# One batch's instruction order in an attention-block kernel: the TensorE, VectorE and ScalarE queues rewritten

## The chip, the cores and the metric

The kernel runs on 1 core of one Trainium2 chip. The metric is the device time of one execution in microseconds (us). Engines: PE is TensorE (PEld its weight loads), DVE is VectorE, ACT is ScalarE, POOL is GpSimd, SP is SyncE, which here only issues DMAs. Each engine works through its own instructions strictly in the order in which the program lists them; semaphores tie the engines together.

## The reference

Two layers over `x` of shape (32, 256, 256). Layer 0 is an attention block with an adaptive norm, layer 1 a response added to its output. Cut to what matters:

```python
# layer 0, B=32 batches, S=D=256, 16 heads of 16
emb = silu(_sin_emb(timestep)) @ W_ada + b_ada;  scale, shift = split(emb)
x = _ln(src) * (1 + scale) + shift
q, k, v = (x @ Wq + bq), (x @ Wk + bk), (x @ Wv + bv)          # 16 heads each
scores = q @ k.T / 4 + attention_bias                           # (32,16,256,256)
probs = softmax(where(src_mask, -inf, scores))
x = x + ((probs @ v) @ Wo + bo)
h = _ln(x) * g2 + beta2
x = x + (_gelu2(h @ W1 + b1) @ W2 + b2)                          # F=1024
# layer 1
U_o, V_o = gram_schmidt(U), gram_schmidt(V)                     # 32 columns each
basis = U_o @ V_o.T
strength = sigmoid(relu(mean(x) @ gate_w1.T + gate_b1) @ gate_w2.T + gate_b2) * sigmoid(safety)
out = x + strength * ((x @ basis) @ basis.T[:, :R] @ resp_w.T + resp_b + safety_bias)
```

## The kernel before

The kernel has two phases. Phase one runs the attention of the 32 batches, one batch per pass of a loop whose body each engine has written out for itself (`body(b, n)` in the blocks of vector, scalar and tensor; the first three and the last batches are unrolled, the middle ones are a hardware loop of two batches, `run_batches`, L110). It writes x after attention to DRAM (`x2_d`). Phase two (`body2`) runs the MLP and the response for the 32 batches. The change lies in phase one and in the last pass that leads over to phase two.

Work of one batch in phase one. Sequence rows lie in two tiles of 128 (qt, kt). Heads are handled one by one, 0 to 15; scores are made in groups of four heads.

- SP loads the attention bias of a batch in two chunks of eight heads into a ring of four slots (`load_bias`); chunk 1 of the next batch when the transposes of the batch before are done, chunk 0 of the batch after next when eight heads of this one are transposed (L315, L324).
- POOL adds the mask into the bias in the ring, in place, four heads at a time (`add_mask`, L430), normalises the x of the next batch (`inv_std`, `normalise_x`), and does parts of one Gram-Schmidt step per batch (`gs_norm`, `gs_update`); 32 batches make the 32 steps. Its order isn't changed.
- PE `scores(b, g)` (L1104) writes four heads' scores into four PSUM banks, which are single: a group waits until DVE has reduced all four heads of the group before. `transposes(b, h)` (L1117) turns the probabilities of head h into one of two PSUM banks (`tp_ps[h % 2]`) and waits for the copy of head h-2 and for head h's exponentials. `pv(b, g)` (L1132) multiplies four heads' transposed probabilities with v, into bank 6. Bank 6 also holds, in turn, the natural-layout context (`ctx_natural`, twice), its transpose (`ctx_transpose`) and the output projection (`project_o`); each of these waits for the eviction of the one before. Bank 7 (`prep_ps`) holds in turn the transposed x, Q, K, V and the transposed-back x of the next batch (`x_transpose`, `project_qk`, `project_v`, `x_back`), and the Gram products (`gs_gram`).
- DVE `reduce_head(b, h)` (L596) adds masked bias to scores, writes the sum to the ring and takes the row minimum of its negative; two instructions and two accumulator reads per head. It also evicts bank 7 (`xT_out`, `q_out` twice, `k_out`, `v_out`, `xres_out`), divides the context by the row sums (`normalise_ctx`, twice), adds the residual (`x2_out`), takes statistics of x (`stats`, `stats_end`), evicts the Gram products, and copies heads 3, 7 and 11 of the transposed probabilities (`copy_pT`, L609).
- ACT `exp_head(b, h)` (L872) does the exponentials in place, two instructions per head; `copy_pT(b, h)` (L879) copies the other 13 heads' transposed probabilities from PSUM to SBUF; `pv_out` and `ctxT_out` evict bank 6; `gs_coefficients`, `gs_write`, `gs_column` belong to the Gram-Schmidt step.

The order of each engine is written by hand as a loop over a slot h from 0 to 15, with one head's work per slot and fixed lags between engines (`behind(b, n, h, k)`, L103: the work of head h-k, reaching into the batch before): DVE reduces head h, ACT exponentiates head h-1, PE transposes head h-3, ACT or DVE copies head h-4. Everything else is hung on a slot number ("if h == 7"). What an engine does in the slot is what another waits for by semaphore count, so counts are independent of the order, and the order alone decides who stands in front of whom.

## Time and profile before

| | us |
|---|---|
| median of 3 runs (lowest, highest) | 1502.5 (1501.99, 1502.88) |
| the profiled execution itself | 1502.05 |
| its span, first to last instruction | 1499.9 |
| PE busy | 1369.4 (91%) |
| PE weight loads busy | 1129.5 (75%) |
| ACT busy | 1086.8 (72%) |
| DVE busy | 1065.5 (71%) |
| POOL busy | 870.4 (58%) |
| mean DMA rate over the span | 116 GB/s |

Phase one ends and phase two begins where the first MLP matmul starts, at 1016.83 us of the span. A matmul's recorded duration reaches to the modelled end of its result, which overlaps the next matmul in an unbroken run.

### The profile page before, as it was taken

The numbers are of one execution on the slowest core, as the hardware profiler recorded it, in microseconds if no ns is written. First come the engines' busy times: TensorE is split into PE (matmuls) and PEld (weight loads), VectorE is DVE, ScalarE is ACT, GpSimd is POOL, SyncE is SP. The second block draws the span as 40 slices with busy tenths as digits, with TensorE's granted clock in tenths as the row PEclk, the third lists the DMA queues.
The fourth block names the chain that finished last, engine by engine and source line by source line (L and its number), as shares of the span: only waits on it lengthen the run. The fifth ranks groups of instructions, "written<-read, shape, count | busy, mean of one in ns | idle before, by whom it ended". The sixth has DMA issues, their size and how long they took to land.

```text
span 1499.9 us, 39676 instructions
## 1 busy us (share of the span) xinstructions
PE 1369.4 (91%) x11998; PEld 1129.5 (75%) x11998; DVE 1065.5 (71%) x3539; ACT 1086.8 (72%) x2696; POOL 870.4 (58%) x874
## 2 busy tenths in 40 slices
PE   3899899999999899989998999989999999999997
PEld 3666666666666666666666666658999999999997
DVE  3667666766676666666666667657888888888775
ACT  1777777777777777777777777777777776777773
POOL 4997878787878787788878887722121212222110
PEclk9999999999999999999999999999999999999999
DMA  7545454545445454545454547200101010111100
GB/s 239 192 129 183 138 181 139 165 153 165 155 149 169 148 172 134 184 134 186 128 186 132 185 135 238 81 22 29 43 28 42 28 42 28 42 34 36 42 22 29
DMA packets 182766, 175.01 MB, mean 117 GB/s; under 512 B 15648, under 2 KB 182208, under 8 KB 182720
## 3 DMA queue, kind: packets, MB, share of 16 engines
q1 hardware_dynamic: 182720, 174.42, 36.7%
q8 instruction: 25, 0.41, 0.1%
q14 instruction: 21, 0.17, 0.0%
HBM read 157.63 MB, written 16.78 MB: 116 GB/s over the span
## 4 chain that ended last, share of the span: by engine, by line
PE 76%; DVE 12%; ACT 5%; issue 4%; SPq 1%; ACTq 1%; DVEq 0%; DMA 0%
PE bank L1323 13%; PE bank L1310 12%; PE bank L1114 9%; PE bank L1129 9%; PE bank L1172 8%; DVE ring L606 5%; PE bank L1152 4%; PE bank L1216 4%; PE bank L1179 4%; PE bank L1356 3%; ACT pT L882 2%; PE bank L1080 2%; ACT ring L877 2%; PE bank L1198 2%; DVE xT L618 2%
## 5 line engine op out<-in xcount | busy, mean ns | idle before, releaser
L430 POOL TENSOR_TENSOR ring<-ring,maskv 128x1024 f32<-128x1024 f32 x256 | 598.4, 2365 | 15.2 <-DMA ring<-in_fside 7.8
L877 ACT ACTIVATE ring<-ring,nmax 128x256 f32<-128x256 f32 x1024 | 458.5, 502 | 115.1 <-DVE nmax L606 112.7
L606 DVE CUSTOM_DVE_ANT_0 ring<-bank,ring 128x256 f32<-128x256 f32 x1024 | 385.5, 417 | 165.3 <-PE bank L1114 163.9
L1129 PE MATMUL bank<-ident,ring 128*128 128x128 f32 x2048 | 306.8, 278 | 26.4 <-ACT pT L882 26.4
L1129 PEld LDWEIGHTS bank<-ident,ring 128*128 128x128 f32 x2048 | 234.4, 142 | 95.2 <-ACT ring L877 42.1
L882 ACT ACTIVATE pT<-bank 128x512 f32<-128x512 f32 x416 | 243.1, 585 | 62.1 <-PE bank L1129 62.1
L984 ACT ACTIVATE work<-bank,b1t 128x256 f32<-128x256 f32 x256 | 107.5, 475 | 114.8 <-PE bank L1310 114.8
L1114 PE MATMUL bank<-work 32*128 32x256 f32 x2048 | 147.5, 402 | 26.3 <-DVE nmax L606 26.3
L1310 PE MATMUL bank<-hT_high,w_high 128*128 128x256 f32 x512 | 153.1, 299 | 3.0 <-DVE hT_rest L763 3.0
L1152 PE MATMUL bank<-pT,vt 128*32 128x256 f32 x2048 | 137.1, 385 | 14.5 <-ACT ctxT L892 13.9
L1323 PE MATMUL bank<-w_high,gT_high 128*128 128x256 f32 x512 | 147.9, 289 | 0.0
L1323 PE MATMUL bank<-w_rest,gT_high 128*128 128x256 f32 x512 | 144.4, 282 | 0.0
L1310 PE MATMUL bank<-hT_high,w_rest 128*128 128x256 f32 x512 | 144.2, 282 | 0.0
L1310 PE MATMUL bank<-hT_rest,w_high 128*128 128x256 f32 x512 | 144.2, 282 | 0.0
L1323 PE MATMUL bank<-w_high,gT_rest 128*128 128x256 f32 x512 | 144.2, 282 | 0.0
L779 DVE SCALAR_TENSOR_TENSOR pT<-work 128x512 f32<-128x512 f32 x128 | 89.3, 698 | 73.1 <-ACT work L988 59.5
L462 POOL TENSOR_SCALAR vpeb<-mvb 128x2 f32<-128x2 f32 x32 | 6.1, 191 | 226.8 <-DVE mvb L693 226.6
L1114 PEld LDWEIGHTS bank<-work 32*128 32x128 f32 x2048 | 92.9, 185 | 55.0 <-DVE nmax L606 41.4
L476 POOL TENSOR_TENSOR work<-work,b2b 128x512 f32<-128x512 f32 x32 | 41.6, 1300 | 131.8 <-DVE work L794 131.8
L1310 PEld LDWEIGHTS bank<-hT_high,w_high 128*128 128x128 f32 x512 | 96.9, 189 | 4.4 <-DVE x2s L662 2.3
L1152 PEld LDWEIGHTS bank<-pT,vt 128*32 128x32 f32 x2048 | 56.0, 109 | 57.9 <-issue 35.6
L376 POOL TENSOR_TENSOR nrm<-gii,expo 128x2 f32<-128x2 f32 x32 | 22.5, 704 | 130.3 <-DVE gsb L574 130.3
(158 smaller groups left out, 2851.2 us busy)
## 6 DMA issues: line engine op xcount, KB each, us to landing
ring<-in_fside SPq DMA_DIRECT2D x128, 1024.0 KB, 7.5
xt<-in_x SPq DMA_DIRECT2D x32, 256.0 KB, 7.8
x_d<-x2s SPq DMA_DIRECT2D x32, 256.0 KB, 7.8
work<-x_d SPq DMA_DIRECT2D x32, 256.0 KB, 2.7
out<-pT SPq DMA_DIRECT2D x32, 256.0 KB, 2.2
mk<-in_mask SPq DMA_DIRECT2D x32, 64.0 KB, 6.6
w<-in_W SPq DMA_DIRECT2D x2, 1024.0 KB, 10.8
wada<-in_W_ada SPq DMA_DIRECT2D x1, 512.0 KB, 4.0
```

Of the source, the lines that this page charges most:

```text
L430: nc.gpsimd.tensor_tensor(v, v, m, ALU.add).then_inc(s_masked, 1)
L606: nc.vector.tensor_tensor_reduce(out=v, in0=score_ps[h % HG][:, qt], in1=v, scale=-1.0, scalar=ROW_MAX_NEG, op0=ALU.add, op1=ALU.min, accu ...
L779: nc.vector.scalar_tensor_tensor(gT[:, 2 * j:2 * j + 2], th[:, j], 1.0, up[:, j], ALU.add, ALU.mult).then_inc(s2_g, 1)
L877: nc.scalar.activation(v, v, ACT.Exp, bias=nmax[:, b.par, h, qt:qt + 1], scale=-1.0).then_inc(s_exp, 1)
L882: nc.scalar.activation(pT[:, h % (2 * HG)], tp_ps[h % 2], ACT.Copy).then_inc(s_pta, 1)
L984: ins = nc.scalar.activation(th[:, j, f], tiles2(j)[:, f], ACT.Tanh, bias=b1t[:, 2 * j + f:2 * j + f + 1], scale=0.5 * GELU_A)
L1114: ins = mm(score_ps[r][:, qt], qm[rows, b.par, a, c, qt * P:(qt + 1) * P], kT[rows, b.par, c], start=True, stop=True)
L1129: ins = nc.tensor.transpose(tp_ps[h % 2][:, kt, qt * P:(qt + 1) * P], ring[:, slot, qt, h % CH, kt * P:(kt + 1) * P], ident[:])
L1152: ins = mm(pv_ps[VW * j:VW * (j + 1), :], vt[:, b.par, kt, h], pT[:, h % (2 * HG), kt], start=(kt == 0), stop=(kt == QT - 1))
L1172: ins = mm(prep_ps[:, n], w[:, c, n * P:(n + 1) * P], xT[:, c], start=(c == 0), stop=(c == DC - 1))
L1310: ins = mm(tiles2(j)[:, f], w1s[kw][:, c, n * P:(n + 1) * P], hTs[kx][:, b.par, c], start=(c == 0 and k == 0), stop=(c == DC - 1 and k == ...
L1323: ins = mm(tiles2(4)[:, t], gTs[kx][:, b.par, f, t * P:(t + 1) * P], w2s[kw][:, f], start=(f == 0 and k == 0), stop=(f == FC - 1 and k == ...
```

## The change

The three bodies (DVE, ACT, PE) are rewritten as straight lists; `behind` goes. What each function does and waits for is the same, and so is the number of instructions. Moved are:

- PE: x_transpose stands first in the batch, scores of group 1 behind head 0's transposes, group 2 behind head 5's, group 3 behind head 8's, group 0 of the next batch behind PV of group 1. The large projections lie between these. PV of group 2 is done at the end of the same batch; x_back stands ahead of the last head's transposes, and the output projection behind head 13's. All 16 heads' transposes are in the batch's own body.
- DVE: heads 0, 1, 2 of the next batch are reduced at the end of a body. The row maxima of a group come as soon as its scores are there, and evictions between them.
- ACT: exponentials of head 0 of the next batch stand in a body's end; copies are ahead of exponentials of heads further off (as copies 1 and 2 ahead of exponentials 4); gs_coefficients comes behind copy 4, gs_write behind exponentials 10.
- The last pass (n == B) has the same pieces in a new order: the output projection of the last batch now comes ahead of the transposes of phase two's first batch and of the last two steps of the response matrix.

```diff
--- before.py
+++ after.py
@@ DVE body @@
+            def reduces(b, heads):
+                for h in heads:
+                    reduce_head(b, h)
+
             def body(b, n):
-                for h in range(H):
-                    if main:
-                        reduce_head(b, h)
-                    at = behind(b, n, h, 4)
-                    if at and at[1] in DVE_HEADS:
-                        copy_pT(*at)
...
+                if n is None or n >= 2:
+                    x2_out(b.plus(-2))
+                if main:
+                    xres_out(b)
+                    if n is None or 1 <= n < B - 2:
+                        stats_end(b.plus(2))
+                    reduce_head(b, 3)
+                if prep:
+                    xT_out(b.plus(1))
+                if main:
+                    reduce_head(b, 4)
+                if tail:
+                    gs_reciprocal(b.plus(-1).n)
+                if main:
+                    reduces(b, (5, 6, 7))
+                    copy_pT(b, 3)
...
+                if prep:
+                    q_out(b.plus(1), 0)
+                    q_out(b.plus(1), 1)
+                if tail:
+                    normalise_ctx(b.plus(-1), 0)
+                if main:
+                    reduce_head(b, 8)
+                if tail:
+                    normalise_ctx(b.plus(-1), 1)
+                if main:
+                    reduce_head(b, 9)
+                if prep:
+                    k_out(b.plus(1))
+                if main:
+                    reduce_head(b, 10)
+                    copy_pT(b, 7)
+                    reduce_head(b, 11)
+                if prep:
+                    v_out(b.plus(1))
...
+                if main:
+                    reduces(b, (12, 13, 14, 15))
+                    gs_products(b)
+                    if n is None or n + 3 < B:
                         stats(b.plus(3))
+                    copy_pT(b, 11)
+                if prep:
+                    reduces(b.plus(1), (0, 1, 2))
...
@@ ACT body @@
+                if main:
+                    exp_head(b, 1)
+                    exp_head(b, 2)
+                    copy_pT(b, 0)
+                    exp_head(b, 3)
+                    copy_pT(b, 1)
+                    copy_pT(b, 2)
+                    exp_head(b, 4)
+                if tail:
+                    pv_out(b.plus(-1), 2)
+                if main:
+                    exp_head(b, 5)
+                if tail:
+                    pv_out(b.plus(-1), 3)
+                if main:
+                    exp_head(b, 6)
+                    copy_pT(b, 4)
+                if tail:
+                    gs_coefficients(b.plus(-1).n)
+                if main:
+                    exp_head(b, 7)
+                    exp_head(b, 8)
+                    copy_pT(b, 5)
+                    copy_pT(b, 6)
+                    exp_head(b, 9)
+                    pv_out(b, 0)
+                    exp_head(b, 10)
+                if tail:
+                    gs_write(b.plus(-1).n)
...
+                if main:
+                    gs_column(b.n)
+                    copy_pT(b, 8)
+                    exp_head(b, 11)
+                    copy_pT(b, 9)
+                if tail:
+                    ctxT_out(b.plus(-1))
+                if main:
+                    exp_head(b, 12)
+                    copy_pT(b, 10)
+                    exp_head(b, 13)
+                    pv_out(b, 1)
+                    exp_head(b, 14)
+                    exp_head(b, 15)
+                    copy_pT(b, 12)
+                    copy_pT(b, 13)
+                if prep:
+                    exp_head(b.plus(1), 0)
+                if main:
+                    copy_pT(b, 14)
+                    copy_pT(b, 15)
@@ PE body @@
+                if prep:
+                    x_transpose(b.plus(1))
+                if main:
+                    transposes(b, 0)
+                    scores(b, 1)
+                    transposes(b, 1)
+                    transposes(b, 2)
+                if prep:
+                    project_qk(b.plus(1), 0)
+                if main:
+                    transposes(b, 3)
+                if tail:
+                    pv(b.plus(-1), 3)
+                if main:
+                    transposes(b, 4)
+                    transposes(b, 5)
+                if tail:
+                    ctx_natural(b.plus(-1), 0)
+                if main:
+                    scores(b, 2)
+                if tail:
+                    ctx_natural(b.plus(-1), 1)
+                if prep:
+                    project_qk(b.plus(1), 1)
+                if main:
+                    pv(b, 0)
+                    transposes(b, 6)
+                    transposes(b, 7)
+                if prep:
+                    project_v(b.plus(1))
+                if main:
+                    transposes(b, 8)
+                    scores(b, 3)
+                    transposes(b, 9)
+                if tail:
+                    ctx_transpose(b.plus(-1), main)
+                if main:
+                    gs_gram(b, n)
+                    transposes(b, 10)
+                    transposes(b, 11)
+                    pv(b, 1)
+                if prep:
+                    scores(b.plus(1), 0)
+                if main:
+                    transposes(b, 12)
+                    transposes(b, 13)
+                if n == B:
+                    response_matrix(0)
+                if tail:
+                    project_o(b.plus(-1), main)
+                if n == B:
+                    y_transpose(Batch(0))
+                    response_matrix(1)
+                if main:
+                    transposes(b, 14)
+                if prep:
+                    x_back(b.plus(1), True)
+                if main:
+                    transposes(b, 15)
+                    pv(b, 2)
+                if n == B:
+                    response_matrix(2)
```

## Rows read from the trace of the kernel before

**Rows 1.** Busy time by stretch: us, then PE, PEld, DVE, ACT, POOL busy, clock, DMA.
```profile
500.00:530.30 30.30, 27.43 (x252) 20.51 (x252) 20.92 (x88) 22.75 (x57) 24.02 (x23) 1.00 0.50 158
...
1032.00:1499.00 467.00, 459.60 (x3802) 449.62 (x3801) 367.22 (x677) 334.52 (x862) 90.23 (x146) 0.99 0.11 34
```

**Rows 2.** Timeline of PE, scores of group 0: start, busy us, engine, line, operation.
```profile
90.66 1.15 PE L1114 MATMUL bank<-work 32*128 32x256 f32 x16
...
969.45 1.15 PE L1114 MATMUL bank<-work 32*128 32x256 f32 x16
```

**Rows 3.** Timeline of PE in one batch of the loop.
```profile
506.45 1.07 PE L1152 MATMUL bank<-pT,vt 128*32 128x256 f32 x16
507.45 0.66 PE L1129 MATMUL bank<-ident,ring 128*128 128x128 f32 x4
508.04 1.15 PE L1114 MATMUL bank<-work 32*128 32x256 f32 x16
...
510.94 0.60 PE L1129 MATMUL bank<-ident,ring 128*128 128x128 f32 x4
511.98 1.07 PE L1152 MATMUL bank<-pT,vt 128*32 128x256 f32 x16 [0.45 <-ACT ctxT L892]
...
513.48 0.60 PE L1129 MATMUL bank<-ident,ring 128*128 128x128 f32 x4
514.42 0.65 PE L1129 MATMUL bank<-ident,ring 128*128 128x128 f32 x4 [0.34 <-ACT pT L882]
515.00 1.15 PE L1114 MATMUL bank<-work 32*128 32x256 f32 x16
516.08 1.99 PE L1216 MATMUL bank<-wo,ctxT 128*128 128x256 f32 x8
517.91 1.04 PE L1129 MATMUL bank<-ident,ring 128*128 128x128 f32 x8
519.91 0.63 PE L1161 MATMUL bank<-ident,xn 128*128 128x128 f32 x4 [0.97 <-DVE xres L647]
...
521.91 0.66 PE L1129 MATMUL bank<-ident,ring 128*128 128x128 f32 x4
522.85 1.15 PE L1114 MATMUL bank<-work 32*128 32x256 f32 x16 [0.28 <-DVE nmax L606]
...
528.22 0.60 PE L1198 MATMUL bank<-ident,pv_sb 128*128 128x128 f32 x4
529.22 0.65 PE L1129 MATMUL bank<-ident,ring 128*128 128x128 f32 x4 [0.40 <-ACT pT L882]
530.31 0.93 PE L1114 MATMUL bank<-work 32*128 32x256 f32 x12 [0.44 <-DVE nmax L606]
```

**Rows 4.** Timeline of DVE in the same batch.
```profile
514.12 0.69 DVE L612 COPY pT<-bank 128x512 f32<-128x512 f32 x1 [0.58 <-PE bank L1129]
516.43 0.42 DVE L606 CUSTOM_DVE_ANT_0 ring<-bank,ring 128x256 f32<-128x256 f32 x1 [1.62 <-PE bank L1114]
...
516.78 0.42 DVE L606 CUSTOM_DVE_ANT_0 ring<-bank,ring 128x256 f32<-128x256 f32 x1
...
518.28 0.69 DVE L662 TENSOR_TENSOR x2s<-bank,xres 128x512 f32<-128x512 f32 x1 [1.08 <-PE bank L1216]
```

**Rows 5.** Timeline of ACT in the same batch.
```profile
514.45 1.70 ACT L877 ACTIVATE ring<-ring,nmax 128x256 f32<-128x256 f32 x4
516.04 0.59 ACT L882 ACTIVATE pT<-bank 128x512 f32<-128x512 f32 x1
```

**Rows 6.** Timeline of POOL in the same batch.
```profile
510.83 0.70 POOL L376 TENSOR_TENSOR nrm<-gii,expo 128x2 f32<-128x2 f32 x1 [3.96 <-DVE gsb L574]
...
522.50 1.06 POOL L386 TENSOR_SCALAR gprod<-coef,qcol 128x32 f32<-128x32 f32 x4 [1.21 <-ACT coef L904]
```

**Rows 7.** POOL's instructions on the ring: count, ns min/median/max, first and last start.
```profile
L430 POOL TENSOR_TENSOR ring<-ring,maskv x256: 2344/2364/2396, 27.7 to 973.4; 128x1024 f32<-128x1024 f32 x128
```

**Rows 8.** The page's DMA issues: count, KB each, median us to landing.
```profile
ring<-in_fside SPq DMA_DIRECT2D x128, 1024.0 KB, 7.5
```

More of the change, by code:

```diff
@@ L100, in copied @@
     return len(heads) * b.n + sum(1 for k in heads if k <= h)
-def behind(b, n, h, k):
-    if h >= k:
-        return (b, h - k) if n is None or n < B else None
-    return (b.plus(-1), h - k + H) if n is None or n >= 1 else None
 def run_batches(eng, first, loop_from, loop_to, last, body):
@@ new lines, in body @@
+                if n == 0:
+                    stats(Batch(2))
+                    stats_end(Batch(2))
+                if n == B:
+                    stats2(Batch(1))
+                if prep:
[9 more added lines that the diff above has]
+                    reduce_head(b, 9)
@@ L752, in _ @@
+                if prep:
+                    reduces(b.plus(1), (0, 1, 2))
+                if n == B:
+                    response_matrix(0)
+                    split_weights(0)
+                    response_matrix(1)
+                    response_matrix(2)
+            reduces(Batch(0), (0, 1, 2))
             run_batches(dve, 0, 3, B - 3, B, body)
@@ L932, in body @@
                 main = n is None or n < B
+                prep = n is None or n + 1 < B
                 tail = n is None or n >= 1
-                for h in range(H):
-                    at = behind(b, n, h, 1)
-                    if at:
-                        exp_head(*at)
-                    at = behind(b, n, h, 4)
-                    if at and at[1] in ACT_HEADS:
-                        copy_pT(*at)
-                    if h == 2 and tail:
-                        gs_coefficients(b.plus(-1).n)
-                    if h == 3 and tail:
-                        pv_out(b.plus(-1), 2)
-                    if h == 5 and tail:
-                        pv_out(b.plus(-1), 3)
-                    if h == 8 and tail:
-                        gs_write(b.plus(-1).n)
-                    if h == 9 and main:
-                        gs_column(b.n)
-                    if h == 11 and main:
-                        pv_out(b, 0)
-                    if n == B and h == 7:
-                        yn_out(Batch(0))
-                    if n == B and h == 10:
-                        split_weights(0)
-                    if h == 12 and tail:
-                        ctxT_out(b.plus(-1))
-                    if h == 14 and main:
-                        pv_out(b, 1)
@@ new lines, in body @@
+                if tail:
[11 more added lines that the diff above has]
+                if n == B:
+                    yn_out(Batch(0))
+                    split_weights(0)
@@ new lines, in body @@
+                if tail:
[10 more added lines that the diff above has]
+                    transposes(b, 13)
+                if n == B:
+                    response_matrix(0)
+                if tail:
+                    project_o(b.plus(-1), main)
@@ L1288, in _ @@
+                if n == B:
+                    y_transpose(Batch(0))
+                    response_matrix(1)
+                if main:
[5 more added lines that the diff above has]
+                    pv(b, 2)
+                if n == B:
+                    response_matrix(2)
             run_batches(pe, 0, 3, B - 3, B + 1, body)
```

88 lines of the change are left out of this document (3 added, 85 removed).

## The prediction

> **What bounds the kernel now.** The page's busy shares put TensorE first; I then read the busy time by stretch [rows 1]. One batch of the attention phase takes 30.3 us: TensorE is busy for 27.4 of them, POOL for 24.0, ACT for 22.8, DVE for 20.9, DMA for half. The MLP phase behind it shows 459.6 busy of 467 us at a granted clock of 0.99, and nothing in it is edited, so only the attention phase can move. Its length per batch is read from the scores of group 0, which start at 90.66 us for batch 2 and at 969.45 for batch 31 [rows 2]: 878.8 / 29 = 30.30 us.
>
> Then the timeline of TensorE in one batch [rows 3]. The reader is to look at distances between starts, not at durations: a head's four transposes are busy for 0.60 us, yet in an unbroken run the next group starts 0.44 later (two heads: 1.04 against 0.60). The "idle before" of a row therefore understates a stall by the end of the last matmul. By starts, I find six losses in this batch:
> - PV of group 1 comes 1.04 behind its transposes, where 0.53 is the pace (PV itself takes 1.00: 506.45 to 507.45; a PV entry costs about 0.1 over the 0.44): 0.51, released by ACT's context copy.
> - transposes at 514.42, 0.94 behind the last ones: 0.50, a probability copy.
> - transposes of x at 519.91, 2.00 behind two heads of 0.44: 1.12, DVE's residual eviction (xres).
> - scores at 522.85, 0.94 behind transposes where 0.59 is the pace (507.45 to 508.04): 0.35, DVE's row maxima.
> - transposes at 529.22, 1.00 behind 0.44: 0.56, a probability copy.
> - scores at 530.31, 1.09 against 0.59: 0.50, row maxima.
> Together 3.54 us. The batch's TensorE work without them is 30.33 - 3.54 = 26.79 us.
>
> **The change part by part.** No instruction is added or removed; three engines' orders change. The transition costs on TensorE stay: before and after, four score groups and four PV groups are entered from wide tiles, but one (scores of the next batch's group 0 now follow PV of group 1 directly), which the rows don't show; I allow -0.1 to +0.3 for it. So TensorE's floor is 26.8, at most 27.0. The question is whether a wait remains. I laid the new order on a clock with the paces of [rows 3]: transposes 0.44 to 0.5, scores 1.07, O 1.83 (516.08 to 517.91), Q and K (the same shapes) too, PV 1.00; the 2.7 left of the 26.79 I give to V (1.75) and Gram (0.95). Starts, x_transpose at 0 (Th, Rh, Eh: transposes, reduction, exponentials of head h; Sg, PVg: scores and PV of group g): T0 0.5, S1 1.1, T1 2.2, T2 2.65, Q 3.1, T3 4.95, PV3 of the batch before 5.45, T4 6.45, T5 6.95, context 0 7.4, S2 8.0, context 1 9.05, K 9.55, PV0 11.45, T6 12.45, T7 12.95, V 13.4, T8 15.1, S3 15.7, T9 16.75, context transpose 17.25, Gram 17.7, T10 18.6, T11 19.05, PV1 19.6, S0 of the next batch 20.7, T12 21.75, T13 22.25, O 22.7, T14 24.5, x_back 24.95, T15 25.45, PV2 25.95, next at 26.95.
>
> Hand-offs: first row maximum 1.41 behind the start of the scores (515.00 to 516.43), an eviction 0.64 behind transposes (513.48 to 514.12), 2.2 behind O (516.08 to 518.28), of which 1.83 are its matmuls [rows 3, 4]; so I take 2.05 behind Q or K and 1.2 behind PV. A head costs DVE 0.69 (two reductions 0.35 apart, 516.43 to 516.78 [rows 4]), an eviction of a full bank 0.6 to 0.7 (0.69 busy), a half bank 0.35 to 0.5. A head costs ACT 0.80 for its exponentials (two heads 1.59, 514.45 to 516.04) and 0.48 for a copy (0.59 busy, a tenth of it under its neighbour, as 1.70 busy stand against 1.59) [rows 5].
>
> DVE, row maxima ahead of evictions: R12-15 run from 17.1 to 19.85, so S0 at 20.7 has 0.8 to spare. Gram products, statistics and copy 11 fill the 1.41 behind S0's start; R0-2 end at 24.15. x2_out waits for O (24.9), xres_out ends 26.4, and x_transpose at 26.95 starts with 0.4 to spare: the largest loss is gone, because O now stands 3.3 before the batch's end and not directly ahead of it. R3 ends at 0.2, 0.9 before S1. xT_out ends 1.6, Q wants it at 3.1. R4-7 follow S1 (2.5 to 5.35), copy 3 and both halves of Q fill the gap to S2, R8 10.1, both context halves are normalised 0.25 and 0.6 before context 1 and PV0 want them, K is out at 12.2 (V: 13.4), R11 ends 14.9 against S3 at 15.7. Four score groups, no wait on any.
>
> ACT: E4 ends 4.6, pv_out(2) 4.9, 0.45 before PV3 wants it. Here ACT idles for PV3 (to 6.65; it costs ACT 0.9), pv_out(3) is done at 7.05, 0.25 ahead of context 0. Second idle: copy 6 waits for T6 until 13.1 (1.8 lost to ACT; queued behind it are exponentials 9 and 10, wanted only at T9 16.75 and T10). The context copy is out at 18.4, PV1 wants it at 19.6 (the 0.51 goes); copies 9, 10, 12, 13 are 0.5 to 1.8 ahead of T11, T12, T14, T15. The copy that T2 needs (head 0) ends 1.75, T2 is at 2.65 (both 0.5s go). PV2 wants x2_out (25.6): 0.2 to spare. These smallest margins, 0.2 to 0.25 in three places, are where a wait may come back.
>
> POOL's code is unmoved, but its loop is the next bound. Busy 24.0, idle 6.3 [rows 1], of which 3.96 wait for the Gram products and 1.21 for ACT's coefficients [rows 6]; the rest, 1.1, is its own hand-offs. Its loop is 25.1 per batch, under 26.8. Afterwards it would wait for the coefficients, which ACT computes at 8.4 to 9.2 instead of beside the third head. Then update, mask, two adds, x and two adds again (14.6) put gs_norm at 23.7 of the batch, 5 us before DVE's reciprocal takes it; masked scores are 6 us ahead of R8. No cost, while the loop stays under 26.8.
>
> SP: the bias loads stand behind T15 and T7 as before. T7 ends about 13.5, landing takes 7.5 [rows 8], POOL's adds on that slot come at 38: nothing. x2's store and the x load are passed in the same order.
>
> The Trainium skill (GPSIMD Engine Reference, Specifications) says that GpSimd shares its SBUF interfaces with VectorE and contends with VectorE instructions that read two SBUF inputs. If denser DVE work stretched the adds, POOL's loop would be the bound. The trace bears it out weakly: the 256 adds lie between 2344 and 2396 ns whatever DVE did beside them [rows 7]. The skill (Perfetto Trace Analysis, Identifying the Most-Contended Engine) would judge TensorE's headroom by weight loads, busy 20.5 of 30.3 [rows 1]; by that, up to 9.8 us per batch would be free. Distances between starts give 3.5, and I go by them.
>
> **Sum.** Steady batches: I take 27.0 (floor 26.8 plus 0.2 for the unseen transition or a small wait): 3.3 x 29 = 96 us. First two batches: they show fewer losses (no context or O work in batch 0), 2 to 6, taken 5. Last batch: without projections TensorE has gaps, ACT and the latency set its pace in either order; PV3 is reached about 1 earlier and O stands ahead of the response matrices: 0 to 4, taken 2. 103 us from the profiled run's 1502.05 (span 1499.9 and 2.15 around it; the median of the runs is 1502.5, 0.45 above): 1399 us.
>
> **Rivals.**
> A. Part of the waits moves rather than goes: a 0.2 margin fails and the copies at the two transpose banks or a score group wait again. For it: ACT at 85% and DVE at 78% of a 26.9 us batch, in strict order. Against: most margins are 0.5 to 1. Half of the 3.54 kept: 28.5 per batch, 1502 - 1.8 x 29 - 5 = 1445; a quarter 1420.
> B. Another floor: POOL's loop 10% longer (27.5), or TensorE held to its busy 27.4 rather than to 26.8. 2.85 x 29 = 83, and 5: 1414. For: POOL has the least room. Against: the even add times and the unbroken paces of [rows 3].
> C. Slower. One loop runs through all engines: pv_out(2), PV3, pv_out(3), context 0, S2, R8, normalise 1, PV0, T6, copy 6, then ACT's work until the next pv_out(2). With bare latencies: 0.5 + 1.2 + 0.5 + 0.6 + 1.4 + 0.7 + 0.8 + 1.0 + 0.65 + 0.5 = 7.85, and ACT's 12 exponentials, 10 copies and small ones, 15.9: 23.75. Above 26.8 it sets the pace, above 30.3 the kernel is slower. It needs 0.73 more at each of nine hand-offs; waits of that size exist (1.08 and 1.62 on DVE [rows 4]). At 0.9 each: 31.85, +1.55 x 29 = 1547. Against: those waits are for work not yet issued, not latency.
> D. No change (a stall outside the reordered code paces the batch, such as loads): DMA is half idle; 1502.
>
> **Chances.** Forecast 0.66 (own range 1383 to 1412), B 0.12, A 0.13, C 0.06, D 0.03. Range 1383 to 1445: it leaves out C, D and the worse part of A. Faster 0.91, same (within 0.2%, about what a measurement of this kernel can tell from no change) 0.03, slower 0.06.
>
> **What would show it.** Scores of group 0 should be 26.8 to 27.2 apart in steady batches; the xres wait before x_transpose, the context-copy wait before PV1 and DVE's row-maximum waits in TensorE's list gone or under 0.2 each; POOL waiting for ACT's coefficients, not for the Gram products; ACT idle before pv_out(3) and copy 6. A is shown by a new releaser in front of T or PV, B by POOL without idle or adds over 2.45 us, C by x_transpose distances over 30. Wrong would be a distance above 28 with TensorE idle.

## The result and the profile after

The changed kernel takes 1390.6 us (median of 4 runs, 1388.91 to 1391.2) against 1502.7 (1501.99 to 1504.35): ratio 0.925, 95% interval 0.9236 to 0.9259. The forecast was 1399, faster. The profiled execution spans 1388.2 us, 111.7 less than before; the sum had 103.

The page's busy line (engine, us, share of the span, instructions):

```profile
PE 1335.7 (96%) x11998; PEld 1126.6 (81%) x11998; DVE 1066.6 (77%) x3539; ACT 1077.6 (78%) x2696; POOL 870.3 (63%) x874
```

The same work in less time: the counts are unchanged, the shares rise. Busy time by stretch, columns as in [rows 1]: one steady batch, then the first 20 us of the MLP phase.

```profile
500.00:526.30 26.30, 26.30 (x254) 20.32 (x253) 20.81 (x88) 22.52 (x57) 24.06 (x23) 1.00 0.56 182
900.00:910.00 10.00, 8.05 (x47) 8.08 (x48) 7.12 (x13) 6.22 (x13) 1.29 (x5) 0.66 0.17 53
910.00:920.00 10.00, 7.98 (x55) 7.78 (x54) 8.89 (x17) 9.13 (x22) 2.18 (x4) 0.83 0.10 28
```

TensorE is busy for all of the batch's 26.30 us, where [rows 1] have 27.43 of 30.30. POOL does the same 24 us of work and has lost only idle time. TensorE's timeline of one batch, as in [rows 3] (start us, busy us, engine, line, operation, "[idle before <-releaser]" where it waited):

```profile
503.34 0.98 PE L1116 MATMUL bank<-uv,ucol 128*128 128x32 f32 x8
504.15 1.07 PE L1165 MATMUL bank<-ident,ring 128*128 128x128 f32 x8
505.15 1.07 PE L1188 MATMUL bank<-pT,vt 128*32 128x256 f32 x16
506.15 1.15 PE L1150 MATMUL bank<-work 32*128 32x256 f32 x16
507.23 1.09 PE L1165 MATMUL bank<-ident,ring 128*128 128x128 f32 x8
508.16 1.89 PE L1252 MATMUL bank<-wo,ctxT 128*128 128x256 f32 x8
509.88 0.60 PE L1165 MATMUL bank<-ident,ring 128*128 128x128 f32 x4
...
511.29 1.07 PE L1188 MATMUL bank<-pT,vt 128*32 128x256 f32 x16
512.29 0.66 PE L1197 MATMUL bank<-ident,xn 128*128 128x128 f32 x4
...
515.32 1.89 PE L1208 MATMUL bank<-xT,wqp 128*128 128x256 f32 x8
517.05 0.60 PE L1165 MATMUL bank<-ident,ring 128*128 128x128 f32 x4
```

No row carries an idle time, and none of the batch's others do; nor does any from batch 2 to the stall described below. The transposes of x stand 1.00 behind PV (511.29 to 512.29), where [rows 3] have 0.97 idle for DVE's residual eviction; PV of group 1 stands 1.00 behind its transposes, without the wait for the context copy; scores of the next batch follow PV directly, 1.00 behind its start.

The other engines are as laid out, DVE at x2_out, ACT at pv_out(3) and at copy 6, POOL at the coefficients:

```profile
510.26 0.69 DVE L655 TENSOR_TENSOR x2s<-bank,xres 128x512 f32<-128x512 f32 x1 [0.53 <-PE bank L1252]
511.05 0.69 DVE L640 TENSOR_TENSOR xres<-bank,bob 128x512 f32<-128x512 f32 x1
```
```profile
518.72 0.38 ACT L896 ACTIVATE pv_sb<-bank 128x256 f32<-128x256 f32 x1 [0.69 <-PE bank L1188]
525.13 0.60 ACT L890 ACTIVATE pT<-bank 128x512 f32<-128x512 f32 x1 [1.82 <-PE bank L1165]
```
```profile
521.35 1.07 POOL L379 TENSOR_SCALAR gprod<-coef,qcol 128x32 f32<-128x32 f32 x4 [1.13 <-ACT coef L912]
```

ACT idles 0.69 and 1.82 where the prediction's layout had 0.9 and 1.8. POOL no longer waits for the Gram products (3.96 in [rows 6]).

**Where the 111.7 us went**, by starts of TensorE's groups. Scores of batch 2's group 0: 85.46 against 90.66 [rows 2], -5.2. The 29 batches from there: 29 x 30.30 before; the scores of batch 31 were due at 847.96, right behind PV, so (847.96 - 85.46) / 29 = 26.29: -116.3. They start 4.7 late, at 852.64 (below). From them to the first MLP matmul 49.3 instead of 47.4: +1.9. From there to the span's end 486.3 instead of 483.1: +3.2. Sum: -111.7.

### The profile page after: what moved, and what is told of

It reads as the page before. It is cut to its first block and busy times, and to the rows that moved or that the text cites. A ratio compares the mean times of both kernels' runs of the same rounds, so it can differ in the third digit from the quotient of the medians.

```text
span 1388.2 us, 39650 instructions
## 1 busy us (share of the span) xinstructions
PE 1335.7 (96%) x11998; PEld 1126.6 (81%) x11998; DVE 1066.6 (77%) x3539; ACT 1077.6 (78%) x2696; POOL 870.3 (63%) x874
## 5 line engine op out<-in xcount | busy, mean ns | idle before, releaser
L885 ACT ACTIVATE ring<-ring,nmax 128x256 f32<-128x256 f32 x1024 | 453.0, 502 | 28.4 <-DVE nmax L599 28.4
L599 DVE CUSTOM_DVE_ANT_0 ring<-bank,ring 128x256 f32<-128x256 f32 x1024 | 373.1, 418 | 91.2 <-PE bank L1150 74.9
L890 ACT ACTIVATE pT<-bank 128x512 f32<-128x512 f32 x416 | 239.5, 592 | 101.6 <-PE bank L1165 101.5
L1165 PE MATMUL bank<-ident,ring 128*128 128x128 f32 x2048 | 293.5, 279 | 1.4 <-ACT pT L890 1.1
L1150 PEld LDWEIGHTS bank<-work 32*128 32x128 f32 x2048 | 93.5, 186 | 37.3 <-issue 28.2
L1361 PEld LDWEIGHTS bank<-hT_rest,w_high 128*128 128x128 f32 x512 | 98.7, 193 | 0.0
L1361 PEld LDWEIGHTS bank<-hT_high,w_rest 128*128 128x128 f32 x512 | 98.2, 192 | 0.0
```

The lines of the kernel that those rows point to most:

```text
L599: nc.vector.tensor_tensor_reduce(out=v, in0=score_ps[h % HG][:, qt], in1=v, scale=-1.0, scalar=ROW_MAX_NEG, op0=ALU.add, op1=ALU.min, accu ...
L885: nc.scalar.activation(v, v, ACT.Exp, bias=nmax[:, b.par, h, qt:qt + 1], scale=-1.0).then_inc(s_exp, 1)
L890: nc.scalar.activation(pT[:, h % (2 * HG)], tp_ps[h % 2], ACT.Copy).then_inc(s_pta, 1)
L1150: ins = mm(score_ps[r][:, qt], qm[rows, b.par, a, c, qt * P:(qt + 1) * P], kT[rows, b.par, c], start=True, stop=True)
L1165: ins = nc.tensor.transpose(tp_ps[h % 2][:, kt, qt * P:(qt + 1) * P], ring[:, slot, qt, h % CH, kt * P:(kt + 1) * P], ident[:])
L1361: ins = mm(tiles2(j)[:, f], w1s[kw][:, c, n * P:(n + 1) * P], hTs[kx][:, b.par, c], start=(c == 0 and k == 0), stop=(c == DC - 1 and k == ...
```

## Two losses that the prediction did not have

**A DVE stall in batch 30.** TensorE there (the second row starts 5.68 behind the first, where 1.00 is the pace):

```profile
846.96 1.07 PE L1188 MATMUL bank<-pT,vt 128*32 128x256 f32 x16
852.64 1.79 PE L1150 MATMUL bank<-work 32*128 32x256 f32 x16 [4.61 <-DVE nmax L599]
```

DVE and POOL beside it, after, and then the same DVE instructions and POOL before:

```profile
843.49 1.54 DVE L668 TENSOR_SCALAR w<-w 128x2048 f32<-128x2048 f32 x1
844.95 2.32 DVE L669 TENSOR_SCALAR b1t<-b1c 128x8 f32<-128x8 f32 x1
...
847.25 2.58 DVE L671 TENSOR_TENSOR cb<-cb 128x256 f32<-128x256 f32 x1
```
```profile
839.26 10.29 POOL L423 TENSOR_TENSOR ring<-ring,maskv 128x1024 f32<-128x1024 f32 x4
```
```profile
962.60 1.22 DVE L675 TENSOR_SCALAR w<-w 128x2048 f32<-128x2048 f32 x1
963.73 0.17 DVE L676 TENSOR_SCALAR b1t<-b1c 128x8 f32<-128x8 f32 x1
...
963.87 0.41 DVE L678 TENSOR_TENSOR cb<-cb 128x256 f32<-128x256 f32 x1
```
```profile
965.32 0.70 POOL L376 TENSOR_TENSOR nrm<-gii,expo 128x2 f32<-128x2 f32 x1 [6.91 <-DVE gsb L574]
```

`constants2()` prepares phase two's constants, once, in batch B-2. In the old order it fell into an idle stretch of POOL and took 1.7 us. In the new one it lies beside POOL's adds and takes 6.3: the 128x8 operation has 2.32 instead of 0.17. The last ends at 849.83, at the end of POOL's four adds (839.26 + 10.29 = 849.55). Row maxima 12 to 15, queued behind it, and with them the next scores, come late. The granted clock falls in the wait: the scores at 852.64 take 1.72 instead of 1.08, and the two heads behind them 1.76 instead of 0.93. The adds pay too, 10.29 for four against 4 x 2.36. The Trainium skill (SBUF — State Buffer, Who interferes with whom) says that GpSimd shares its ports with VectorE's second pair under an exclusive lock. By the same section of the Trainium skill a VectorE instruction contends when it runs in a two-port mode, which tensor_scalar can enter, or when it has two SBUF inputs, as `cb + cb2` has; the later one then waits for the whole of the other. By it, too, one with a single SBUF input outside these modes does not contend. The trace agrees on both sides. 2.32 is one add's length for an operation of 0.17. The statistics of x, which also read and write SBUF alone, are not held: all 64 lie close together (ns min/median/max), the two at 505.70 among them, while POOL adds from 505.07 to 509.77.

```profile
L502 DVE BATCH_NORM_STATS2 st<-xt x64: 402/412/427, 3.7 to 795.3; 128x6 f32<-128x256 f32 x64
```

The prediction looked only at the adds' side of this. The even add times of [rows 7] were no test even of that: in the steady batch every VectorE tensor_scalar and tensor_tensor has a PSUM bank among its operands.

**The MLP's start.** Granted clock 0.66 and 0.83 between 900 and 920 us after; 0.77 and then 1.00 in the first 16 us before. In the last pass in front of it TensorE's idle times are up to 1.6 us before and up to 2.9 after, but they don't explain it. Three of the experiments below (one more pair saved, the output projection late, ACT with an even lag), all of them new orders, have 0.79 and then 1.00, and take 483.1 to 483.4 us from the first MLP matmul to the end, as before. The other nine have 0.59 to 0.70 in the first 8 us and take 484.7 to 488.3. So the 3.2 us follow how soon the granted clock rises in an execution, and nothing here ties that to the order of phase one. What decides it stays open.

## The experiments

All are edits of the changed kernel; "after" was run again beside the first ones: 1390.7 (1388.98 to 1392.08), ratio 0.9246 [0.9229, 0.9263], again 26.29 to 26.30 per batch.

> The changed kernel once more, as the base for the three runs beside it. Both theories: 1390.6 us within 1.5, scores of group 0 of neighbouring batches 26.30 us apart.

**The constants moved** into the last pass:

```diff
                 if n == B:
                     stats2(Batch(1))
+                    constants2()
...
-                if n == B - 2:
-                    constants2()
```

> Edit: DVE's one-off scaling of MLP constants (four instructions) moves from the last but one batch, between head 11's and head 12's row maxima, to the last pass, behind the statistics of MLP batch 1. Theory 1: in the changed kernel two of the four, a 128x8 one of 2.32 us and a 128x256 one of 2.58 us, waited for POOL's adds, where the kernel before shows 0.17 and 0.41 with POOL idle; behind them the scores of batch 31 started 4.7 us late and then ran at half clock. In the last pass POOL and DVE have idle time: the rows fall back to under 0.5 us each, the 4.7 go and some 1.5 of the half clock, 1384 to 1385 us. Rival: the time only moves, since the last pass is a chain of latencies in which DVE stands at the end: 1389 to 1391 us.

1385.0 (1383.16 to 1386.46), ratio 0.921 [0.9193, 0.9227]. The scores stand directly behind PV (845.89, 846.89), and the operations that took 2.32 and 2.58 take 0.17 and 0.42, POOL being idle there:

```profile
877.17 0.17 DVE L669 TENSOR_SCALAR b1t<-b1c 128x8 f32<-128x8 f32 x1
...
877.31 0.42 DVE L671 TENSOR_TENSOR cb<-cb 128x256 f32<-128x256 f32 x1
```

The stall was theirs, and moving it away is worth 5.7 us. By the profiles it was 4.7 of wait and 1.4 of half clock behind it: from the scores of batch 31 to the first MLP matmul it is now 47.9 instead of 49.3.

**What a change between narrow and wide groups costs.** Head 12's transposes put between PV of group 1 and the next scores:

```diff
+                    transposes(b, 12)
                 if prep:
                     scores(b.plus(1), 0)
                 if main:
-                    transposes(b, 12)
                     transposes(b, 13)
```

> Edit: head 12's transposes move from behind the next batch's scores of group 0 to between PV of group 1 and those scores. No wait should arise (head 10's copy ends 0.5 us ahead of it). Theory 1, entries: the TensorE work of a batch fell from 26.79 to 26.30 us because the neighbours of the narrow groups changed: scores entered from PV cost no 0.15, and Q, O and Gram behind transposes take 1.73, 1.72 and 0.81 where they took 1.83, 1.83 and 0.91 behind scores. Then this edit costs 0.15 us per batch, 26.45, and 4.7 us in all: 1395 us. Rival: the order of groups is free on TensorE and the 0.49 was hidden waiting in the batch before; then 26.30 and 1390.6 us.

1392.8 (1392.64 to 1394.65), ratio 0.9261 [0.9244, 0.9278]; 26.44 per batch, +0.15. Its timeline:

```profile
504.68 1.07 PE L1188 MATMUL bank<-pT,vt 128*32 128x256 f32 x16
505.68 0.65 PE L1165 MATMUL bank<-ident,ring 128*128 128x128 f32 x4
506.26 1.15 PE L1150 MATMUL bank<-work 32*128 32x256 f32 x16
507.34 0.66 PE L1165 MATMUL bank<-ident,ring 128*128 128x128 f32 x4
```

One head between two narrow groups takes 0.58 instead of 0.44. The Trainium skill (TensorEngine Tiling (Array Packing), Key Properties) says that a change of tiling mode drains TensorE. The trace puts 0.14 us on a pair of changes by way of a wide group; the direct change from PV (128x32) to scores (32x128) shows no price, since PV keeps its 1.00. The medians differ by 2.1, less than the 0.15 x 31 = 4.6 that the period gives, but the profiled span (1390.6) is 3.8 above that of the repeat run beside it (1386.8). The rest is within what executions of one kernel differ by here, some 3 us.

**One more pair of changes saved**, scores of group 2 directly behind PV of group 3:

```diff
                     pv(b.plus(-1), 3)
                 if main:
+                    scores(b, 2)
                     transposes(b, 4)
                     transposes(b, 5)
                 if tail:
                     ctx_natural(b.plus(-1), 0)
-                if main:
-                    scores(b, 2)
-                if tail:
-                    ctx_natural(b.plus(-1), 1)
                 if prep:
                     project_qk(b.plus(1), 1)
+                if tail:
+                    ctx_natural(b.plus(-1), 1)
                 if main:
-                    pv(b, 0)
                     transposes(b, 6)
                     transposes(b, 7)
+                    pv(b, 0)
```

(DVE reduces head 9 ahead of the second context half.)

> Edit: scores of group 2 directly behind PV of group 3 of the batch before; then heads 4 and 5, context 0, K, context 1, heads 6 and 7, PV of group 0; on DVE head 9 ahead of the second context half. Theory 1, entries: one more scores group is entered from PV (0.15 less), K is entered from a transpose (0.1 less), but V now stands behind PV (0.1 more): 26.1 to 26.2 us per batch, 1385 to 1388 us, if no wait comes back; the second context half ends only 0.1 us ahead of PV of group 0 by my clock, so up to 0.3 us of wait per batch may eat it. Rival, order is free on TensorE: 26.30 and 1390.6 us.

Missed: 1396.1 (1395.69 to 1401.13), ratio 0.9291 [0.927, 0.9312], 26.55 per batch. Scores do enter directly (520.80 to 521.80, 1.00), but a wait appears for ACT's copy of head 5:

```profile
526.41 0.60 PE L1164 MATMUL bank<-ident,ring 128*128 128x128 f32 x4
527.16 0.65 PE L1164 MATMUL bank<-ident,ring 128*128 128x128 f32 x4 [0.15 <-ACT pT L889]
```

By starts it is 0.75 - 0.44 = 0.31, and the entry behind it pays 0.05 more (0.58). The order by itself saves only 0.10: the pair and a cheaper K, less 0.10 for V, which now stands behind PV (1.83 instead of 1.73). Together +0.26. I had moved heads 6 and 7 from behind PV to ahead of it, a microsecond nearer to ACT. The margins of the new order are as small as its clock had them.

**Old orders put back in part.** TensorE's or DVE's whole old order alone wasn't tried: each engine would stand in front of what the other needs first.

DVE's evictions of Q around head 5's maxima, not behind copy 3:

```diff
+                if prep:
+                    q_out(b.plus(1), 0)
                 if main:
-                    reduces(b, (5, 6, 7))
+                    reduce_head(b, 5)
+                if prep:
+                    q_out(b.plus(1), 1)
+                if main:
+                    reduces(b, (6, 7))
                     copy_pT(b, 3)
```

> Edit: on DVE alone, the two halves of Q are evicted where the kernel before had them, around head 5's row maxima (behind heads 4 and 5), instead of behind head 7's. Same instructions. Theory 1 (row maxima ahead of evictions is worth something because the scores banks are single and TensorE has no slack): Q is ready about 5.15 us into the batch, so heads 5 to 7 end at 8.5 instead of 5.4, copy 3 at 9.2, and head 5's transposes on TensorE, wanted at 6.95, wait 2.3 us: 28.6 us per batch, 1390.6 + 2.3 x 31 = 1462 us, with TensorE's idle time put down to head 3's copy or to head 5's exponentials. Rival (DVE has idle time, its order is free): under 1395 us.

1502.4 (1501.2 to 1506.23), ratio 0.9992 [0.9978, 1.0005]: two evictions in other places, and all of the gain is gone. DVE stands before Q (first row), copy 3 ends at 528.57, and TensorE waits for it, then runs scores at half clock:

```profile
524.50 0.75 DVE L618 SCALAR_TENSOR_TENSOR work<-bank,half,bqm 128x512 f32<-128x512 f32 x1 [1.67 <-PE bank L1211]
...
527.89 0.68 DVE L605 COPY pT<-bank 128x512 f32<-128x512 f32 x1
```
```profile
528.70 0.65 PE L1168 MATMUL bank<-ident,ring 128*128 128x128 f32 x4 [2.22 <-DVE pT L605]
...
529.93 2.09 PE L1153 MATMUL bank<-work 32*128 32x256 f32 x16
```

The wait costs 2.87 - 0.49 = 2.4 by starts: batches at full clock are 28.72 apart. In most the granted clock falls behind the wait, scores take 2.02 instead of 1.08, and the batch 30.30. Over 200 us the clock is 0.95:

```profile
500.00:700.00 200.00, 186.70 (x1694) 141.71 (x1694) 140.01 (x586) 150.00 (x370) 162.96 (x150) 0.95 0.49 155
```

So my 1462 had the wait right and lacked the clock, 1.6 us in most batches. The Trainium skill (TensorE: Matmul & The Clock Gate, HAM oscillation) describes such a kernel: idle that recurs on TensorE brings back its lower clock each time. The trace agrees, with shorter idle than in the page's example: one stretch of 2.2 us per batch goes with it.

The output projection back behind x_back:

```diff
-                if tail:
-                    project_o(b.plus(-1), main)
...
                 if main:
                     transposes(b, 14)
                 if prep:
                     x_back(b.plus(1), True)
+                if tail:
+                    project_o(b.plus(-1), main)
```

> Edit: on TensorE alone, the output projection moves from behind head 13's transposes to behind x_back, so that it stands 2.5 us instead of 4.3 ahead of the next batch's x_transpose. Theory 1 (the distance from O through x2_out and xres_out to x_transpose is what removed the largest loss): x2_out can end only 2.9 us behind O's start; PV of group 2 waits about 0.7 to 1.0 us for it and x_transpose about 0.5 to 0.8 more: 27.5 to 28.0 us per batch, 1428 to 1445 us, waits on x2_out and xres in TensorE's list. Rival (other changes removed it, DVE has the room): 1391 us.

1436.2 (1434.28 to 1438.62), ratio 0.9563 [0.9547, 0.9579], 27.84 per batch, clock 1.00. PV of group 2 now waits for bank 6, 0.71 in this batch (second row); the row names ACT's copy, but the list of waits has DVE's x2_out waiting for the projection up to 2.2:

```profile
502.74 0.65 PE L1165 MATMUL bank<-ident,ring 128*128 128x128 f32 x4 [0.56 <-ACT pT L890]
506.70 1.07 PE L1188 MATMUL bank<-pT,vt 128*32 128x256 f32 x16 [0.71 <-ACT pT L890]
```
```profile
DVE x2s L655 <- PE bank L1252: 15.2, 7, 2.2
```

That is 1.30 - 0.53 = 0.77 by starts, half of the 1.55 per batch. The other half has nothing to do with x2_out: head 14's transposes (first row) wait for ACT's copy of head 12, which the projection had given time, 1.64 - 0.93 = 0.71. The wait at x_transpose that I had expected did not come.

ACT's four small coefficient operations ahead of exponentials 3, nothing else:

```diff
                     copy_pT(b, 0)
+                if tail:
+                    gs_coefficients(b.plus(-1).n)
+                if main:
                     exp_head(b, 3)
...
                     copy_pT(b, 4)
-                if tail:
-                    gs_coefficients(b.plus(-1).n)
```

> Edit: in the changed kernel only gs_coefficients (four small ScalarE instructions) moves, from behind head 4's copy to ahead of head 3's exponentials, near its old place. Theory 2: ScalarE stands still until DVE's reciprocal, 3.3 us into the batch, and everything behind it shifts: head 3's transposes wait 0.7 us, PV of group 3 another 1.0: 28.0 us per batch at full clock, 1443 us, and up to 1500 if the granted TensorE clock falls in these idle times as in the run where Q was evicted early. Rival (only the sum of moves mattered): under 1400 us.

1440.4 (1435.17 to 1442.01), ratio 0.9575 [0.9555, 0.9595], 28.1 to 28.2 per batch. ACT stands 1.5 us before them with its exponentials behind, and TensorE waits 0.7 and 0.8 to 0.9 per batch, at a clock of 1.00:

```profile
517.83 0.30 ACT L911 ACTIVATE qcol<-ucol,rnrm 128x2 f32<-128x2 f32 x1 [1.53 <-DVE rnrm L571]
```

ACT's whole old order (coefficients at slot 2, pv_out at slots 3, 5, 11 and 14, exponentials one and copies four slots behind):

```diff
+                for h in range(H):
+                    at = behind(b, n, h, 1)
+                    if at:
+                        exp_head(*at)
+                    at = behind(b, n, h, 4)
+                    if at and at[1] in ACT_HEADS:
+                        copy_pT(*at)
+                    if h == 2 and tail:
+                        gs_coefficients(b.plus(-1).n)
+                    if h == 3 and tail:
+                        pv_out(b.plus(-1), 2)
...
```

> Edit: ScalarE's whole order as in the kernel before (exponentials of head h-1, copy of head h-4 per slot), TensorE and VectorE as changed. Theory 1 (copies ahead of far exponentials is a part of its own, but a small one): head 0's copy comes behind head 3's exponentials, and head 2's transposes wait some 0.5 us, further ones 0 to 0.5: 26.8 to 27.5 us per batch, 1405 to 1425 us, waits on ScalarE's copies in TensorE's list. Rival A (ScalarE's order is free, it idles 3.8 us per batch): under 1394 us. Rival B (it carries the gain): over 1450 us.

Missed by 280 us: 1702.1 (1700.6 to 1703.62), ratio 1.1331 [1.1312, 1.135], 200 slower than the kernel before. Batches are 34.8 to 37.8 apart. ACT, then TensorE:

```profile
509.17 0.29 ACT L918 ACTIVATE qcol<-ucol,rnrm 128x2 f32<-128x2 f32 x1 [4.32 <-DVE rnrm L578]
...
518.57 0.38 ACT L903 ACTIVATE pv_sb<-bank 128x256 f32<-128x256 f32 x1 [4.38 <-PE bank L1167]
```
```profile
511.48 0.65 PE L1144 MATMUL bank<-ident,ring 128*128 128x128 f32 x4 [3.48 <-ACT pT L897]
...
513.93 3.13 PE L1187 MATMUL bank<-xT,wqp 128*128 128x256 f32 x8
```

I had priced each early operation's wait alone. They add, as I read it, since what an operation waits for (the reciprocal, the PV) is itself late by the wait before it; and Q takes 2.97 at half clock instead of 1.73.

**ACT with an even lag**: coefficients and pv_out about at their new places, copies three heads behind exponentials in a plain loop. In the steady batch exponentials and copies follow one another exactly as in the experiment before; only the few other operations have moved:

```diff
+                for h in range(H):
+                    if h >= 3:
+                        if main:
+                            exp_head(b, h)
+                        done = h - 3
+                        if main and done in ACT_HEADS:
+                            copy_pT(b, done)
+                    if h == 4 and tail:
+                        pv_out(b.plus(-1), 2)
...
```

> Edit: on ScalarE alone, exponentials and copies go back to the even lag of the kernel before (exponentials of head h, then the copy of head h-3), but the evictions of bank 6 and gs_coefficients, gs_write, gs_column stay about where the changed kernel has them (coefficients behind head 4's copy). Theory 2 (what ScalarE's old order cost in the run before, 36 us per batch, lay in two blocks: gs_coefficients ahead of head 3's exponentials, waiting 4.3 us for a reciprocal that DVE now does behind head 4's maxima, and pv_out of group 3, 4.4 us, and in the half clock that followed; 'copies ahead of far exponentials' by itself is worth nothing, since ScalarE idles 3.8 us per batch): 26.3 to 26.5 us per batch, 1390 to 1397 us. Rival (the order of copies against exponentials is what counts): over 1405 us, waits on ScalarE's copies in TensorE's list.

1398.8 (1393.04 to 1400.28), ratio 0.9306 [0.9293, 0.9319]; 26.48 per batch, no wait in TensorE's list over 200 us. So the fine interleaving of copies and exponentials is worth 0.2 us per batch, and the 303 us between this run and the one before come from the places of the few operations with partners on other engines. Here the constants stall grows, as ACT's copy stands behind an exponential that waits for the late maxima:

```profile
854.53 0.91 ACT L885 ACTIVATE ring<-ring,nmax 128x256 f32<-128x256 f32 x2 [7.15 <-DVE nmax L599]
```

The profiled execution is the shortest of the six (1393.0, mean granted clock 0.991). The others take 4 to 7 us more and have 0.986 to 0.989; where their clock was lower stays open.

**POOL as the next bound**: two 128x512 additions per batch on POOL, on data that nobody uses.

```diff
+                    nc.gpsimd.tensor_tensor(junk[:], maskv[:, 0:1].to_broadcast([P, 2, S]), maskv[:, 1:2].to_broadcast([P, 2, S]), ALU.add)
                     add_mask(b, 0)
...
                     gs_norm(b.plus(-1).n)
+                    nc.gpsimd.tensor_tensor(junk[:], maskv[:, 0:1].to_broadcast([P, 2, S]), maskv[:, 1:2].to_broadcast([P, 2, S]), ALU.add)
```

> Edit: two additions of 128x512 elements into a tile that nothing reads are added on GpSimd per batch, about 1.3 us each by the one such addition that the MLP phase has (1.30 us). Theory 1 (GpSimd's loop is the next bound: it idles 1.13 us per batch, waiting for ScalarE's coefficients): the loop grows to 25.2 + 2.6 = 27.8 us, over TensorE's 26.3: 1.5 us per batch, about 1437 us, GpSimd without any idle time and DVE waiting for masked scores. Rival (its work is far enough ahead, it only uses up a lead): under 1394 us.

1419.4 (1416.67 to 1419.45), ratio 0.944 [0.9424, 0.9456]. The first batches stay at 26.29 while POOL's lead is used up, later ones are 27.65 apart. POOL's groups (count, busy us, mean ns, idle before):

```profile
L423 POOL TENSOR_TENSOR ring<-ring,maskv 128x1024 f32<-128x1024 f32 x256 | 598.9, 2368 | 5.5 <-DMA ring<-in_fside 5.5
...
L442 POOL TENSOR_TENSOR junk<-maskv 128x512 f32<-128x512 f32 x32 | 41.0, 1282 | 2.6
```

25.1 + 2 x 1.28 = 27.7: rival B's loop of 25.1 was read rightly, and it leaves 1.2 us per batch under today's 26.3. The adds keep their 2368 ns beside a POOL that never rests. The total is 18 us under the 1437 that I had expected: the first five batches cost nothing, and the constants do not stall here (0.43 and 0.41 us; the scores of batch 31 start 27.3 behind those of batch 30, instead of 31.0).

**A DVE operation on SBUF alone added**, once per batch behind v_out:

```diff
+                if main:
+                    nc.vector.tensor_scalar(junk[:], ident[:, 0:8], 0.5, None, ALU.mult)
```

> Edit: one DVE instruction is added per batch, a scaling of 128x8 elements from SBUF to SBUF, behind v_out, where POOL is adding masks. Theory 1 (a DVE instruction that has only SBUF operands waits until POOL's running add has ended): its mean duration is 0.8 to 2.3 us, and the scores of group 0, 0.65 us ahead of need plus 0.98 of idle time, come later by 0 to 0.7 us per batch: 1391 to 1412 us. Rival (the two long rows in the changed kernel waited for loads or for each other): 0.1 to 0.2 us each and 1391 us.

1391.0 (1389.25 to 1391.96), ratio 0.9251 [0.9238, 0.9264]: free. Its group (ns min/median/max), one of it, and the adds beside it:

```profile
L744 DVE TENSOR_SCALAR junk<-ident x32: 163/587/593, 56.7 to 874.6; 128x8 f32<-128x8 f32 x32
```
```profile
502.18 0.59 DVE L744 TENSOR_SCALAR junk<-ident 128x8 f32<-128x8 f32 x1
```
```profile
498.06 4.69 POOL L423 TENSOR_TENSOR ring<-ring,maskv 128x1024 f32<-128x1024 f32 x2 [0.17 <-POOL maskv L413]
```

The adds end at 502.75, the operation at 502.77: it is held until the running add ends. It takes 0.59 and not up to 2.4 because it stands at the same place of the cycle each time, shortly ahead of the add's end; I had treated that as chance. DVE still idles 0.47 us behind it (0.98 without it), so it costs nothing.

**Both losses mended**: constants in the last pass, and there ACT's context copy ahead of `yn_out` and `split_weights(0)`:

```diff
-                if n == B:
-                    yn_out(Batch(0))
-                    split_weights(0)
...
                 if tail:
                     ctxT_out(b.plus(-1))
+                if n == B:
+                    yn_out(Batch(0))
+                    split_weights(0)
```

> Edit: the constants' scaling in the last pass as in the run before (measured 1385.0), and in the last pass ScalarE evicts the transposed context ahead of normalising the first MLP batch and of splitting W1, where it made TensorE wait 2.9 us ahead of the last output projection. Theory: the chain from the last projection to the first MLP matmul ends some 2 to 3 us sooner: 1382 to 1384 us. Rival: DVE's splitting of W1, which waits for ScalarE's, ends the chain instead and comes 0.6 us later: 1385 to 1386 us.

1382.3 (1380.02 to 1384.54), ratio 0.9194 [0.9179, 0.921], the fastest of all. The last output projection, which waited 2.86 for that copy (first row, after), does not wait (second row, this kernel). From the scores of batch 31 to the first MLP matmul it is now 45.1, against 47.9 with the constants alone moved:

```profile
893.48 3.35 PE L1252 MATMUL bank<-wo,ctxT 128*128 128x256 f32 x8 [2.86 <-ACT ctxT L900]
```
```profile
883.44 3.41 PE L1251 MATMUL bank<-wo,ctxT 128*128 128x256 f32 x8
```

## Why the prediction was right, and where its sizes were off

- **The six losses go, none comes back**: right. Q's evictions, the coefficients and the output projection, put back one at a time, each bring waits back and cost 112, 50 and 45 us; these do not add up to the gain, since each alone delays the whole cycle.
- **Steady batches, 96 us**: measured 116. The term mis-sized is the floor, 27.0 (26.8 and 0.2 for unseen things) against 26.29. The 0.2 wasn't needed (no small wait, x_transpose 1.00 behind PV), and "-0.1 to +0.3" for the new entry to scores had the wrong centre: that entry saves a pair of changes, 0.14 by the head-12 experiment. "The transition costs on TensorE stay" was wrong beyond that entry. Q went from 1.83 (523.92 to 525.75) to 1.73, O from 1.83 to 1.72, Gram from 0.91 to 0.81, as they stand behind transposes and no longer behind scores. With K and V these take 7.81 instead of 8.13 by starts, 0.32 less; the transposes between take the other 0.18 less, the saved pair among it.
- **First batches, 5**: 5.2, but the same order gives 5.2 to 6.7 in four executions, so the closeness is in part luck. **Last batch, 2 gained**: 1.9 lost. Of this 1.4 is the half clock behind the constants' stall, and 2.8 the wait for ACT's context copy, which stood behind phase two's first work; without both, 45.1 us against 47.4 before is a gain of 2.3. So TensorE's order there gives what I took for it, and what I left out was ACT's order and the once-only work.
- **Nothing in the MLP phase moves**: 3.2 lost to a granted clock that is lower for longer at its start. Three runs of new orders don't lose them, so the term is one of the execution and not, as far as shown, of the change.
- **The total, 103 against 111.7**: 20 us too few in the steady batches and some 12 us of losses that I didn't have in part cancel.
- **No once-only work was costed**: the constants, 4.7 at the scores of batch 31 and 5.7 in all. The argument "DVE's maxima are early" holds for the steady batch only.
- **Margins**: one was not as laid out. DVE waits 0.54 for POOL's add ahead of head 0's maxima (at 507.58 in this batch), a lead of POOL's that I hadn't laid out for that head. It costs nothing, since the maxima are still in time.
- **Rivals**: B (POOL's loop) is the next bound, at 1.2 us from here; TensorE's floor was its distances between starts, not its old busy time of 27.4. The Trainium skill's view by weight loads (Perfetto Trace Analysis, Identifying the Most-Contended Engine) would still see room: 20.32 of 26.30, on a TensorE that waits for nothing. A and C did not occur here, but with ACT's old order the batches are 34.8 to 37.8 apart, slower than before, as C had it for a loop through all engines; that it is C's loop, hand-off by hand-off, isn't shown.

## What to carry to other kernels

Where strict queues are tied together, lay one period of all engines on a clock with start-to-start paces, and place first the few operations with a partner on another engine; the bulk between them may follow a plain lag (0.2 us per batch here). Then walk the same clock through the first, last and once-only passes, since a tighter cycle moves them beside other work. Look at the granted clock too when a wait stays on TensorE: here one wait of 2.4 us per batch, by starts, cost up to 1.6 more by the clock.

## What the runs showed of the hardware

- A DVE tensor_scalar from SBUF to SBUF and a tensor_tensor with both inputs in SBUF are held while a POOL addition runs: 2.32 and 2.58 us instead of 0.17 and 0.41, and 0.59 instead of 0.16, ending with the add. The reductions, which read PSUM and SBUF, keep 0.41 to 0.42 beside the same adds, and the batch-norm statistics, with one input and that in SBUF, 0.40 to 0.43.
- TensorE pays 0.14 us for one wide group between two narrow ones, and nothing for scores directly behind PV.
- With one wait of 2.2 us per batch the granted clock was 0.95 on average, with waits of up to 3.5 it was 0.90; with waits of up to 0.9 (coefficients early, output projection late) it stayed at 1.00.
